# Attention row maxima in a fused attention and expert block: turned by VectorE instead of TensorE, and taken bank by bank

## What is computed

```
xn = layernorm(x)
# attention, 16 heads of 16; each projection is of low rank: 32 numbers per row
q, k, v = holo_linear(xn, basis, phase, amp)         # (xn @ basis.T) @ (amp * cos(phase)).T
p = softmax(q @ k.T / 4)                             # per head, 512 x 512
attn = holo_linear(p @ v, ...)
# experts: top 2 of 8 by softmax, scaled 2.5, silu(x @ wg) * (x @ wu) @ wd, F = 352
# and a shared expert of width 704 for all rows
out = x + attn + experts + shared
```

## Time and profile before

| | |
|---|---|
| median of 3 runs | 946.4 us (944.36 to 946.92) |
| the profiled execution's own time | 944.99 us |
| its span, first to last instruction | 943.2 us |
| mean granted clock of TensorE over the span | 0.97 |
| instructions | 19555 |
| moved by DMA | 133.74 MB, mean 142 GB/s |

### The profile page before, as it was taken

The page is one execution under the profiler, slowest core; times in us unless marked ns, Lnnn a source line. Parts: engine busy times, 40 slices in busy tenths (PEclk is TensorE's granted clock), DMA queues, the critical chain, the costliest instruction groups (busy, mean ns, idle before and its releaser), DMA issues.

```text
span 943.2 us, 19555 instructions
## 1 busy us (share of the span) xinstructions
PE 871.3 (92%) x6491; PEld 605.1 (64%) x6492; DVE 608.0 (64%) x914; ACT 583.3 (62%) x941; POOL 427.3 (45%) x417
## 2 busy tenths in 40 slices
PE   5846999999999989889999999999999999999996
PEld 2436999999999976456556555555565465565462
DVE  6787844444444455676786786786777877776752
ACT  5855744444444442767767767767767866856764
POOL 2104722222222151753753764854754844744831
PEclk9965999999999999999999999999999999999997
DMA  9884555222222216554854755755755655654310
GB/s 315 315 265 149 187 151 172 72 72 68 76 67 69 65 47 171 157 154 101 203 158 118 198 159 127 198 155 130 189 163 130 192 161 130 191 141 109 76 48 23
DMA packets 91479, 133.74 MB, mean 142 GB/s; under 512 B 17512, under 2 KB 51824, under 8 KB 91024
## 3 DMA queue, kind: packets, MB, share of 16 engines
q1 hardware_dynamic: 84720, 114.95, 43.3%
q0 software_dynamic: 6480, 17.70, 7.1%
q10 hardware_dynamic: 208, 0.14, 0.0%
HBM read 76.10 MB, written 51.56 MB: 135 GB/s over the span
## 4 chain that ended last, share of the span: by engine, by line
PE 80%; DVE 11%; issue 3%; ACT 2%; DMA 2%; POOL 1%; DVEq 0%; ACTq 0%; POOLq 0%
PE bank L1463 12%; PE bank L1503 10%; PE s_pair L1412 9%; PE bank L1359 8%; PE s_pair L1341 8%; PE bank L1568 7%; PE st_pair L1491 6%; PE st_pair L1341 6%; DVE top L1934 4%; PE bank L1349 2%; PE bank L1324 2%; DMA xg<-xn_rows,token_of 1%; PE bank L1476 1%; PE bank L1517 1%; PE bank L1402 1%
## 5 line engine op out<-in xcount | busy, mean ns | idle before, releaser
L1934 DVE TENSOR_REDUCE top<-s_pair 128x2 f32<-128x1024 f32 x248 | 303.7, 1225 | 134.1 <-PE s_pair L1412 131.2
L1120 ACT ACTIVATE prob<-st_pair 128x1024 f32<-128x1024 f32 x252 | 259.1, 1028 | 116.9 <-PE st_pair L1491 109.1
L780 POOL DMA_INDIRECT xg<-xn_rows,token_of x71 | 82.7, 1165 | 207.5 <-PE bank L1324 157.3
L1463 PE MATMUL bank<-xT_b,w_sh 64*128 64x512 f32 x960 | 143.2, 404 | 0.5
L1412 PE MATMUL s_pair<-k_rows,q_rows 48*128 48x512 f32 x496 | 115.6, 459 | 12.0 <-DVE top L1934 11.8
L1503 PE MATMUL bank<-prob,v_ones 128*32 128x512 f32 x1024 | 124.8, 605 | 0.0
L1463 PEld LDWEIGHTS bank<-xT_b,w_sh 64*128 64x128 f32 x960 | 91.7, 187 | 31.1 <-issue 8.3
L1491 PE MATMUL st_pair<-q_rows,k_rows 50*128 50x512 f32 x504 | 106.2, 415 | 3.4 <-ACT prob L1120 2.6
L1359 PE MATMUL bank<-w_exp,c_hT 128*128 (+1 forms) x639 | 94.2, 292 | 0.6 <-ACT c_y L1027 0.6
L1412 PEld LDWEIGHTS s_pair<-k_rows,q_rows 48*128 48x128 f32 x496 | 47.4, 184 | 64.9 <-DVE top L1934 55.4
L1341 PE MATMUL s_pair<-w_exp,xg_T 128*128 x468 | 88.1, 338 | 0.0
(11 more groups left out here) (238 smaller groups left out, 1240.6 us busy)
## 6 DMA issues: line engine op xcount, KB each, us to landing
qk_rows<-qk_hi SPq DMA_DIRECT2D x56, 256.0 KB
q_rows<-qk_rows SPq DMA_DIRECT2D x64, 192.0 KB
k_rows<-qk_rows SPq DMA_DIRECT2D x56, 192.0 KB
expert_rows<-c_y SPq DMA_DIRECT2D x71, 128.0 KB, 1.7
qk_rows<-qk_lo SPq DMA_DIRECT2D x28, 256.0 KB
x_all<-in_L_attn_x_dram SPq DMA_DIRECT2D x8, 512.0 KB, 7.3
xn_rows<-x_n SPq DMA_DIRECT2D x8, 512.0 KB, 3.5
o_b<-in_L_attn_x_dram SPq DMA_DIRECT2D x8, 512.0 KB, 6.5
```

Of the source, the lines that this page charges most:

```text
L780: pool.indirect_dma_start(xg[s % 4][:, :], None, xn_dram, bass.IndirectOffsetOnAxis(token_of[:, s:s + 1], 0)).then_inc(c_x[s % 4], 16)
L1120: act.activation(prob[n % 3][:, 2 * jp:2 * jp + 2, :].rearrange("p j l -> p (j l)"), score_T_pair(b, g, t)[:, :], ACT.Exp, scale=HD ** -0. ...
L1463: ins = pe.matmul((g_bank, u_bank)[up][:, :], w_sh[rows, a, o:o + P], xT_of(b)[rows, c, k, :], start=(n == 0 and i == 0), stop=(n == 1 and ...
L1934: dve.tensor_reduce(top[g % 2][:, :, jp, qt], score_pair(b, g, v)[:, :].rearrange("p (i k) -> p i k", i=2), AX_X, ALU.max).then_inc(d_max, 1)
```

## The change

Four DVE transposes of 32 by 32 take the place of PE's turn and ACT's copy. Each maximum becomes two reductions of 512 columns, one per bank, with its own count, and each of the two score products waits for the reduction of its own bank. The users of `m_bank` that waited for ACT's copy wait for the user before that instead. `top_T` is written by DVE.

```diff
             def load_max(b, g):
-                wait(sp, a_mt, b * NG + g + 1)
+                wait(sp, d_mt, b * NG + g + 1)
...
-            def max_rows(b, g):
-                wait(act, b_mt, b * NG + g + 1)
-
-                wait(act, m_in[g % 2], (2 * b + g // 2) * 32)
-                act.activation(top_T[g % 2][:, :], m_bank[0:32, 0:P], ACT.Copy).then_inc(a_mt, 1)
-
...
                 elif n == 1:
-                    wait(pe, a_mt, (b - 1) * NG + 2)
+                    wait(pe, d_qk, b * 4 + 1)
                 elif n == 2:
                     wait(pe, a_v, (b - 1) * 2 + 2)
                 else:
-                    wait(pe, a_mt, (b - 1) * NG + 3)
+                    wait(pe, d_qk, b * 4 + 3)
...
             def score(b, g, v):
-                wait(pe, d_max, b * 32 + g * 8 + v)
+                free = b * 32 + g * 8 + v
                 for i in range(2):
                     r = 64 * i
-                    ins = pe.matmul(score_pair(b, g, v)[:, i * 512:(i + 1) * 512], q_rows[g][r:r + 48, jp, qt * P:(qt + 1) * P], k_rows[g][r:r + 48, jp, :],
-                                    start=True, stop=True)
-                ins.then_inc(b_s, 1)
-
-            def turn_max(b, g):
-                wait(pe, d_m, b * NG + g + 1)
...
-                pe.transpose(m_bank[0:32, 0:P], top_parts[g % 2][:, :, :, :, :].rearrange("p i a j t -> p (i a j t)").bitcast(F32),
-                             ident_f[:, :]).then_inc(b_mt, 1)
+                    if free >= 1:
+                        wait(pe, d_max, free * 2 - 1 + i)
+                    pe.matmul(score_pair(b, g, v)[:, i * 512:(i + 1) * 512], q_rows[g][r:r + 48, jp, qt * P:(qt + 1) * P], k_rows[g][r:r + 48, jp, :],
+                              start=True, stop=True).then_inc(b_s, 1)
...
             def maximum(b, g, v):
                 qt, jp = v // 2, v % 2
-                wait(dve, b_s, b * 32 + g * 8 + v + 1)
                 if v == 0:
                     wait(dve, d_m, b * NG + g - 1)
-                dve.tensor_reduce(top[g % 2][:, :, jp, qt], score_pair(b, g, v)[:, :].rearrange("p (i k) -> p i k", i=2), AX_X, ALU.max).then_inc(d_max, 1)
+                for i in range(2):
+                    wait(dve, b_s, (b * 32 + g * 8 + v) * 2 + i + 1)
+                    dve.tensor_reduce(top[g % 2][:, i, jp, qt:qt + 1], score_pair(b, g, v)[:, i * 512:(i + 1) * 512], AX_X, ALU.max).then_inc(d_max, 1)
 
             def split_max(b, g):
...
                 dve.tensor_tensor(dst[:, :, LO, :, :], src, dst[:, :, HI, :, :].bitcast(F32), ALU.subtract).then_inc(d_m, 1)
+                wait(dve, d_m, b * NG + g + 1)
+                wait(dve, m_in[g % 2], (2 * b + g // 2) * 32)
+                for r in range(0, P, 32):
+                    ins = dve.transpose(top_T[g % 2][:, r:r + 32], dst[r:r + 32, :, :, :, :].rearrange("p i a j t -> p (i a j t)").bitcast(F32))
+                ins.then_inc(d_mt, 1)
```

More of the change, by code:

```diff
@@ L261, in build_program @@
         top_parts = [sb(f"top_parts{i}", [P, 2, 2, 2, TPB], F32R, late) for i in range(2)]
-        top_T = [sb(f"top_T{i}", [32, P], F32R, late) for i in range(2)]
+        top_T = [sb(f"top_T{i}", [32, P], F32, late) for i in range(2)]
         xT_bs = [xT_b, xT_1]
@@ L343, in build_program @@
         inv_in = sem("inv_in")
[L345 to L351, removed]
+        b_r, b_v, b_qk, b_s, b_st, b_pv, b_gu, b_ha, b_res, b_dn, b_po = (
+            sem(f"b_{n}") for n in ("r", "v", "qk", "s", "st", "pv", "gu", "ha", "res", "dn", "po"))
+        a_r, a_v, a_qk, a_exp, a_th, a_uh, a_hh, a_ot, a_ao, a_res = (
+            sem(f"a_{n}") for n in ("r", "v", "qk", "exp", "th", "uh", "hh", "ot", "ao", "res"))
+        d_r, d_qk, d_max, d_mh, d_m, d_mt, d_ga, d_hb, d_inv, d_res, d_dn, d_po = (
+            sem(f"d_{n}") for n in ("r", "qk", "max", "mh", "m", "mt", "ga", "hb", "inv", "res", "dn", "po"))
         b_to, b_bo, d_to, a_bo, d_bo = (sem(n) for n in ("b_to", "b_bo", "d_to", "a_bo", "d_bo"))
@@ L1152, in slot @@
                         up_half(c, q)
-                    if t == 5 and there(nb):
-                        max_rows(nb, ng)
                     if now:
@@ L1484, in score_T @@
                 if (b, g) == (LAST, 3) and t:
-                    wait(pe, d_max, NB * 32)
+                    wait(pe, d_max, NB * 64)
                     wait(pe, a_exp, b * 32 + g * 8 + t - 1)
@@ L1510, in low_rank @@
                 wait(pe, xT_in, 16) if b == 1 else wait(pe, p_xl, b - 1)
-                if b <= 2:
-                    wait(pe, a_mt, 1 if b == 1 else 4)
+                if b == 1:
+                    pe.wait_ge(c_hed, NS - 1)
+                elif b == 2:
+                    wait(pe, d_qk, 8)
                 else:
@@ L1524, in project_values @@
                     wait(pe, r_in, b * 48 + 48)
-                    wait(pe, a_mt, b * NG + 1)
-                    if b == 0:
-                        pe.wait_ge(d_r, 2)
+                    wait(pe, d_r, b + 2) if there(b + 1) else wait(pe, d_po, (b - 1) * 2)
                 elif there(b + 1):
@@ L1530, in project_values @@
                 else:
-                    wait(pe, a_mt, b * NG + 2)
+                    wait(pe, a_v, b * 2 + 1)
                 for t in range(TPB):
@@ L1670, in slot @@
                         values(b, g, 1)
-                    if t == 4 and there(nb):
-                        turn_max(nb, ng)
                     if (g, t) == (1, 0) and now:
```

23 lines of the change are left out of this document (5 added, 18 removed).

## The result

The kernel after took 954.28 us (median of 5, 953.66 to 957.15), the kernel before on the same chip 946.4 (944.36 to 948.04): ratio 1.0092, 95% interval 1.0070 to 1.0114 (worked out from all the runs; the two medians alone give 1.0083). On a second chip the same two gave 1.0128 (1.0099 to 1.0156). Slower, as forecast, by 7 to 15 us instead of 17.5; the time lies in the range. The profiled execution has a span of 955.3 against 943.2, 12.1 more. It was the slowest of the five (957.15 us), and the one profiled before was 1.4 us under its median, so 12.1 is more than the 7.9 between the medians.

A forecast was written before the change was run, and what follows sets the result against it. PE was taken to bound the kernel, with DVE feeding it. Typical groups +9.4, held +4.6, before "down" pieces +2.4, first and last groups -0.5, halves +1.6 gave +17.5 on 945.0: 962.5 us, 8-in-10 range 946 to 975.

The forecast's parts named there:

- step 4: Fourth step of a group, after the last maximum: DVE's new work makes its maximum and gate 1.15 us late.
- PE's saved 0.21: PE's removed transposes, 0.21 us each, at most 6.7 us; in typical groups this falls into the wait for the gate.
- the sum of the prediction: For the turn on DVE behind the split: four transposes of 0.19, gaps and a lost overlap, 0.99 us per group.
- Rival B: No difference: transposes overlap as other DVE neighbours do, 0.63 us late at step 4; +2.5, 947.5 us; 13%.
- rival A: Faster: release by bank clears maxima from PE's way, the turn hides in DVE's slack; 934.5 us; 14%.
- Rival C: Slower still: POOL holds the transposes as it does the cast, +12.3, 974.8 us; 13%.
- held group: Group where POOL holds the split: the whole 1.15 us of lateness is paid; 4 such groups, +4.6 us.
- the halves: Maxima in two reductions: second score product waits 0.08 us longer in about a third of 64 half slots, +1.6 us.
- I: DVE's lateness at the end of step 4, turn plus two halved maxima: 1.15 us, low bound 0.63, high 1.39.
- my own case: Main forecast, 60%: 962.5 us, with its own range of 955 to 970 from transposes of 0.17 to 0.25.
- the high bound: Transposes of 0.25 us each, DVE 1.39 us late at step 4: +24.7, 969.7 us.
- the -0.5: First group, last group and two of the last batch: PE's 0.21 comes through in part, -0.5 us together.

The follow-up runs named there:

- 9: The kernel after with all four transposes of a group moved together behind the gate of step 4: ratio to before 0.9994 (0.9967 to 1.0021).
- 5: The kernel after with four more transposes per group into a spare tile, in the same place: ratio to before 1.0395 (1.0357 to 1.0433).
- kernel 3: The kernel after with whole maxima of two banks and one release, only the turn on DVE: ratio to before 1.0195 (1.0156 to 1.0234).
- 8: The kernel after, step 3 corrections behind step 5's maximum, load_max before stores: 1.0203; with whole maxima 1.0270; with load_rows early too 1.0249.
- 1: The kernel before with maxima in halves and release by bank, turn still on PE and ACT: ratio to before 0.9997 (0.9974 to 1.0021).

## Why the prediction was right in sign and too large

- **Where it is lost: right, and shown.** The loss is DVE's lateness at the maximum and gate of step 4. Undoing only the place (9) undoes it; doubling what stands there (5) adds its full length. The prediction hoped for nothing from PE's saved 0.21 in a typical group, because it falls into the wait; 9 shows that even without that wait nothing of it is left.
- **The transposes: right.** 0.200 each, 0.84 for four, and 0.91 from 585.98 to 586.89 with the gaps; with the lost overlap of 0.08 that is 0.99, the sum of the prediction to the hundredth: each piece is 0.01 longer than taken, the gaps together 0.04 less. Rival B (they overlap) and rival A fall. Of the Trainium skill's rule ("VectorE: DVE Perf Modes", section "Two Vector instructions with no wait between them") the rows agree with more than the prediction used: the transposes, which begin in another group of partitions each, never overlap; the correction behind them, which reads SBUF from partition 0, starts 0.03 behind their end; and in 9 the maximum behind them, which reads only PSUM, starts 0.07 ahead of it (580.38 against 579.61 + 0.84). No run turns the maxima from one group of partitions only, so that it is the group and not the operation that keeps the four apart is not shown.
- **Rival C fell.** No transpose of 128 took over 205 ns, though 33 of them lie wholly under a product of POOL, as these four do.

```profile
603.01 1.29 POOL L810 TENSOR_TENSOR h_T<-h_f,h_T 128x512 fp32r<-128x512 f32 x1
603.11 0.84 DVE L1921 STREAM_TRANSPOSE top_T<-top_parts 32x32 f32<-32x32 f32 x4
```

The Trainium skill ("GPSIMD Engine Reference", section "8. Key points") says that VectorE instructions with two SBUF inputs, or in a 2-port mode, contend with GpSimd; the held subtraction has two SBUF inputs and the transpose has one, and the rows agree. The CAST, which was held as well, reads one; whether it ran in a 2-port mode no row tells.
- **By slot.** Forecast +0.55, +0.55, +0.85 (a typical and a held group in turn), +0.34 and 0.2 for the halves, 2.49 a batch. Measured +0.26, +0.60, +0.84, +0.19: 1.89. Slot 2 came out right through holds in other groups than the ones named: with DVE late, each of POOL's holds is paid in full wherever it falls, and that was said of fixed groups only.
- **The step that failed: the halves.** "PE works in order and the second product waits for the second half", and so I charged 1.6 us for tight steps and put 0.16 into I. With it failed "Nothing later in the slot has room to win it back, since PE is full": the shared product came 0.52 late and the slot ended 0.25 late. The wait is real, but it does not hold up PE as it did: the late product runs beside the first one of score_T, and the early one has gone ahead in what had been a gap. Without the turn the halves came out at -0.15 a batch and with one release at +0.82. In the sum of the prediction they make 2.49 - 1.65 = 0.84 of a batch. On top of the turn they measured 71.55 - 72.08 = -0.5, or nothing (71.55 against 71.51) with the clock's loss taken off kernel 3. Over seven to eight batches 0.8 is 6 us, the size of the miss in the profiled executions (17.5 - 12.1 = 5.4). Against the medians the miss is larger (962.5 - 954.28 = 8.2), and that rest is not traced to a term.
- **Not in the sum:** the first slot, 2.0 us longer with its stretch at half clock, and the last batch and the tail, 2.5 us shorter where 0.5 was forecast. They cancel nearly, and that they do is luck.
- **Slips in the range.** The low end of my own case, 955, is not what a transpose of 0.17 gives: with I = 1.07 the same sum is 17 x 0.47 + 4 x 1.07 + 7 x 0.26 - 0.5 + 1.6 = 15.2, 960.2 us. The measured 954.28 lies below that, and is covered only by the wider range of 8 in 10. The sum at the high bound leaves out the -0.5: 969.2, not 969.7.

Open: what lengthens slot 2 in 8; why PE falls to half clock at 380 us in the kernel after and not in the one before; and how much of the clock's loss in each kernel is on the path, which subtracting it takes as all. PE had idled ahead of each such stretch that I followed, but in 1 and 9 by only 0.21 and 0.22 us, and no run was made with the idle time alone.

## What to carry to other kernels

Work moved to an engine with a quarter of its time free still costs its length, less what is in hand (0.65 us here), if it is put in front of the one result that another engine is about to need; the same instructions a few places later in the queue, behind that result, cost nothing here. They gained nothing either: what the first engine saves can be lost at the next result that the second one owes it. So look for the place before the engine. When a pair of products is released bank by bank, ask what can run beside the late one before charging its wait. And when an edit loses more than its waits add up to, lay the granted clock along the span: in most of the edits here short idle times of PE were followed by stretches at half clock, in which 1.7 to 14 us of PE's time went in all.

## What was not expected of the hardware

- Waits of PE of 0.2 to 2.5 us for an exponent, a maximum or a landing were followed by some 3 to 10 us with the granted clock at half in several kernels, while a wait of 1.00 us (694.94 in the kernel after) or 1.33 us (379.39 before) was not.
- DVE's subtraction of two SBUF tiles was stretched from 0.17 to 1.23 us by one POOL product, while of the halved maxima (74 of which lie wholly under a product of POOL) none took over 694 ns, and no transpose over 205.
- Two reductions of 128x512 take 1.27 to 1.29 us together where one of 128x1024 takes 1.21 to 1.23, 0.06 more; 0.08 had been charged.
